# A graph layer on one core: the counts of a chunk's first three banks are made among the last products of the chunk in front of it

## The reference, cut to what matters

```python
N, D, E = 6250, 128, 206250            # nodes, features, edges; dst is sorted
msg = x[src] + edge_attr
agg = jax.ops.segment_sum(msg, dst, num_segments=N)
h = jax.nn.relu(agg @ W1 + b1) @ W2 + b2
h = norm_over_all(h) * ln_w + ln_b      # one mean and variance for the whole of h
h = norm_over_nodes(h) * gn_w + gn_b    # per feature
y = x + jax.nn.gelu(h) + x
out = layernorm(y)                      # per node
...
```

## Time and profile before

| | us |
|---|---|
| median of 3 runs (853.66 to 855.56) | 854.31 |
| profiled execution, its own time | 847.83 |
| its span, first to last instruction | 845.7 |
| one chunk, counts and products | 25.1 |
| of it from first to behind the last of the 98 products | 11.5 |

### The profile page before, as it was taken

One profiled execution on the slowest core, in us unless ns is written; L12 is line 12 of the kernel. 1 busy time (PEld: TensorE's weight loads), 2 busy tenths in 40 slices (PEclk: granted clock), 3 DMA queues, 4 the chain that ended last, 5 costly groups with the idle time before them and its releaser, 6 DMA issues.

```text
span 845.7 us, 25816 instructions
## 1 busy us (share of the span) xinstructions
PE 731.9 (87%) x9449; PEld 616.1 (73%) x9449; DVE 677.6 (80%) x1189; ACT 380.7 (45%) x841; POOL 84.8 (10%) x67
## 2 busy tenths in 40 slices
PE   3566789999999999999999999999999999989840
PEld 3564458777888877888877788877788887778730
DVE  5766678988988988898898898898898898815585
ACT  0120024566444466544466644456644446615464
POOL 1121001011011011011011101111101101000000
PEclk9997769999999999999999999999999999999965
DMA  6759994554334555333555333455433355212005
GB/s 156 276 169 353 359 349 150 158 158 123 113 117 123 155 158 150 101 113 114 154 158 158 116 114 106 139 158 158 130 106 118 122 155 158 80 66 94 0 1 152
DMA packets 88855, 123.45 MB, mean 146 GB/s; under 512 B 8479, under 2 KB 84348, under 8 KB 88635
## 3 DMA queue, kind: packets, MB, share of 16 engines
q1 hardware_dynamic: 78992, 112.83, 42.9%
q0 software_dynamic: 5616, 5.25, 2.2%
q10 hardware_dynamic: 4228, 5.12, 2.0%
HBM read 119.10 MB, written 4.03 MB: 146 GB/s over the span
## 4 chain that ended last, share of the span: by engine, by line
PE 56%; ACT 19%; issue 10%; DMA 8%; DVE 5%; ACTq 1%; DVEq 1%; SPq 0%
PE bank L696 35%; ACT counts L521 17%; DMA edges<-in_edge_attr_dram 6%; PE bank L674 6%; PE bank L623 5%; PE bank L638 3%; PE bank L743 3%; PE bank L753 2%; DMA agg<-in_dst_dram 1%; PE bank L658 1%; ACT sums L491 1%; PE bank L596 1%; DVE pool_m L1192 1%; DVE pool_m L829 1%; ACTq L519 1%
## 5 line engine op out<-in xcount | busy, mean ns | idle before, releaser
L521 ACT CAST counts<-bank 128x490 fp32r<-128x490 f32 x625 | 311.5, 615 | 291.9 <-PE bank L674 289.1
L696 PE MATMUL bank<-counts,x_hi 128*128 128x250 f32 x1225 | 289.1, 281 | 19.6 <-ACT counts L521 19.6
L696 PE MATMUL bank<-counts,x_lo 128*128 128x250 f32 x1225 | 286.5, 279 | 0.0
L696 PEld LDWEIGHTS bank<-counts,x_hi 128*128 128x128 f32 x1225 | 231.3, 189 | 23.5 <-ACT counts L521 23.5
L980 DVE TENSOR_TENSOR pool_m<-listing,turned_lo 128x3328 bf16<-128x3328 bf16 x125 | 235.9, 1887 | 8.4 <-ACT turned_key L501 7.0
L696 PEld LDWEIGHTS bank<-counts,x_lo 128*128 128x128 f32 x1225 | 232.1, 189 | 0.0
L674 PE MATMUL bank<-pool_m 128*128 128x98 bf16 x3125 | 200.8, 209 | 0.0
L674 PEld LDWEIGHTS bank<-pool_m 128*128 128x128 bf16 x3125 | 158.9, 98 | 46.8 <-issue 45.0
L623 PE MATMUL bank<-edges,onehot 128*32 128x128 f32 x3228 | 171.4, 305 | 22.4 <-DMA edges<-in_edge_attr_dram 22.4
L980 DVE TENSOR_TENSOR pool_m<-listing,turned_key 128x2548 bf16<-128x2548 bf16 x125 | 184.7, 1478 | 0.0
L623 PEld LDWEIGHTS bank<-edges,onehot 128*32 128x32 f32 x3228 | 78.4, 117 | 55.9 <-issue 21.8
(11 more groups left out here) (149 smaller groups left out, 414.3 us busy)
## 6 DMA issues: line engine op xcount, KB each, us to landing
edges<-in_edge_attr_dram SPq DMA_DIRECT2D x134, 768.0 KB, 4.6
out_dram<-pool_m SPq DMA_DIRECT2D x6, 512.0 KB
agg<-in_dst_dram SPq DMA_DIRECT2D x1, 768.0 KB
agg<-in_src_dram ACTq DMA_DIRECT2D x1, 768.0 KB
listed<-agg ACTq DMA_DIRECT2D x1, 768.0 KB
begins<-listed,tile_slot POOLq DMA_INDIRECT x27, 5.8
begins<-listed,row_slot POOLq DMA_INDIRECT x27, 3.4
w<-in_L_gnn_W_dram ACTq DMA_DIRECT2D x2, 128.0 KB, 2.2
```

The source lines that it names most:

```text
L521: nc.scalar.copy(counts[:, :, k * nodes:(k + 1) * nodes].rearrange("p q (i m) -> p q i m", m=PAIR), cps[k % RING][:, 0:nodes * NT].rearran ...
L696: last = nc.tensor.matmul(sps[:, 0:CHUNK], part[:, q, :], counts[:, q, :], start=(q == 0 and part is x_hi), stop=(q == NT - 1 and part is ...
```

## The change

PE makes the counts of banks 0, 1 and 2 of chunk c+1 not at the start of that chunk, but in front of the tiles 40, 43 and 46 of the 49 tiles of chunk c's products. The banks are the same three PSUM banks, the waits are the same, and ACT's and DVE's programs are not touched. For the first chunk the three banks are counted ahead of the loop. The last chunk, behind which nothing follows, is written out of the loop.

```diff
+PREFILL_AT = (40, 43, 46)
...
-            def count_chunk(c):
+            def count_bank(c, k):
+                b = k // BPB
+                if k % BPB == 0:
+                    pe.wait_ge(marks_ready, c * BATCHES + (b + 1))
+                if k >= RING:
+                    pe.wait_ge(banks_free, c * BANKS + (k + 1 - RING))
+                for i in range(BANK):
...
+                last.then_inc(banks_done, 1)
+
+            def count_chunk(c, ahead=True):
                 for k in range(BANKS):
...
+                    if k >= len(PREFILL_AT):
+                        count_bank(c, k)
                     if k in PARTS_AT:
...
                 for q in range(NT):
+                    if ahead and q in PREFILL_AT:
+                        count_bank(c + 1, PREFILL_AT.index(q))
                     for part in (x_hi, x_lo):
...
-            with pe.Fori(0, CHUNKS) as c:
+            for k in range(len(PREFILL_AT)):
+                count_bank(0, k)
+            with pe.Fori(0, CHUNKS - 1) as c:
                 count_chunk(c)
+            count_chunk(CHUNKS - 1, ahead=False)
```

More of the change, by code:

```diff
@@ L663, in _ @@
                 round_groups(r)
-            def count_chunk(c):
-                for k in range(BANKS):
[L667 to L679, removed]
+            def count_bank(c, k):
[5 more added lines that the diff above has]
+                for i in range(BANK):
+                    n = (k % BPB) * BANK + i
+                    last = nc.tensor.matmul(cps[k % RING][:, i * KEYS:(i + 1) * KEYS],
+                                            mark_lo[b % MARKED][:, n // INTER, :, n % INTER],
+                                            mark_key[b % MARKED][:, n // INTER, :, n % INTER],
+                                            start=(i == 0), stop=(i == BANK - 1),
+                                            skip_group_check=True)
+                last.then_inc(banks_done, 1)
+            def count_chunk(c, ahead=True):
+                for k in range(BANKS):
+                    if k >= len(PREFILL_AT):
+                        count_bank(c, k)
                     if k in PARTS_AT:
```

## The result

| | before | after |
|---|---|---|
| median of 11 runs, us | 854.31 (852.79 to 856.17) | 858.48 (856.69 to 862.29) |
| profiled execution, its own time | 847.83 | 857.90 |
| span | 845.7 | 855.8 |
| one chunk, mean of 23 | 25.09 | 25.51 |

The change made the kernel slower: ratio 1.0058 (95% interval 1.0041 to 1.0074), 4.2 us by the medians. The two profiled executions are 10.1 us apart. The forecast was 9.6 us more and 863.9, with a range of 857 to 873.

What follows compares the result with a forecast made beforehand. PE was taken to bound the products, ACT the counts with PE nearly a bound. Gaining 0.59 and paying 0.99 us lengthens each of 24 chunks by 0.40: 854.31 + 9.6 = 863.9 us, own range 861 to 867, wide 857 to 873.

Steps and rivals of the forecast that it cites:

- The sum: Whole kernel: each chunk gains 0.59 and pays 0.99, so 0.40 longer; over 24 chunks 9.6 us, giving 863.9.
- the forecast's own range: Kernel time 861 to 867 us, for x from 0.11 to 0.16; chance 0.60.
- the wide range: Kernel time 857 to 873 us, the forecast's own range widened by rivals 1, 2 and 3 to reach 8 in 10.
- rival 1: Product's weight load hidden behind the count products: x = 0.05, 0.16 a chunk, 858.1 us; chance 0.14.
- x: On PE, the step from a group's fifth count product to the next product; taken as 0.13 us, bounds 0.05 to 0.25.
- The price: Three groups of count products among PE's products: 0.33 us each, 0.99 a chunk, bounds 0.75 to 1.35.
- my two middle cases: Product's weight load starts with the last count product (x = 0.11) or once that has streamed (x = 0.16).
- The gain: Counts phase: 0.21 at ACT's first copy and 0.38 over thirteen copies, 0.59 us a chunk; bounds 0.45 to 0.74.
- Passed on whole: After copy 12 the order is untouched, so the whole 0.59 us reaches the next products.
- drained array: Rival 2: the array drains at each return to the products, x = 0.25, 0.76 a chunk, 872.5 us; chance 0.11.
- Rival 3: Among the copies nothing is won; only the start's 0.21 comes through, 0.78 a chunk, 873.0 us; chance 0.05.
- Rival 5: Faster: the pause around bank 14, 0.51 above the pace, goes as well, -0.11 a chunk, 851.7 us; chance 0.04.

Runs made afterwards that it cites:

- the two later comparisons: No edit: the changed kernel timed again against the kernel before on two later occasions; 858.29 us, ratio 1.0119, and 857.50 us, ratio 1.0108.
- the three later occasions: The kernel before, unchanged, timed again on three occasions, each on another chip: 848.64, 848.81 and 848.26 us.
- alone: Against the kernel before, banks 0 to 2 counted among the products and again at the chunk's start, so only the cost is there: 871.57 us, ratio 1.0267.
- the run with the gain alone: Against the kernel before, counts of banks 0 to 2 left out for chunks 1 to 24 (output not the layer's): 836.93 us, ratio 0.9864.

## Why the prediction was right, and where it was off

- **The sum.** Forecast 0.40 a chunk, measured 25.51 - 25.09 = 0.42, in three profiles of the changed kernel. Over 24 chunks 10 us, as the profiles and the two later comparisons (1.0119 and 1.0108, so 9 to 10 us) have it. The first comparison's 4.2 us was half of that. The step that it doesn't fit is "854.31 + 9.6": the median that I added to was 5 to 6 us above what the same kernel took on the three later occasions. I had noted the gap to the profiled 847.83 and took it to be there after the change as well; it was not (858.48 against a profiled 857.90).
- **Luck.** The measured 858.48 lies outside the forecast's own range of 861 to 867. Only the wide range held it, by 1.5 us, and that range reached down to 857 for the sake of rival 1, whose 858.1 is the nearest figure of all although its mechanism (x = 0.05) is ruled out. Had I added to the profiled execution, as the prediction also did (857.4), or to the later medians (848.3 to 848.8, so 857.9 to 858.4), the mechanism would have given the measured time. The mechanism is borne out by the chunks; that 858.48 lay in the range is owed in part to luck.
- **The price.** 0.99 forecast, 0.95 measured, alone and in the changed kernel. The group was 0.20 + x with x = 0.13; x is 0.11, the lower of my two middle cases, which takes off 0.06 for three groups, and the step out of the products is 0.13 (450.20 to 450.33) in place of 0.12, which gives about 0.03 back. The rule of the Trainium skill on the load ("TensorE: Matmul & The Clock Gate", section "LDWEIGHTS (loading the stationary operand)") gave 0.107 for this step: the trace agrees, with 0.11. Its other rule, in the section "What overlaps and what doesn't" (a load overlaps only matmuls in other row groups), doesn't hold here: the product's load starts at 450.53 beside the last count product, in the same full array.
- **The gain.** 0.59 forecast, 0.53 measured: the first copy 0.40 behind the last product in place of 0.36 (before 0.57), and the thirteen copies in 6.41 in place of 6.39 (before 6.77). ACT needs 0.12, not 0.08, from the end of the last product (453.52 to 453.64). The 0.04 for the wait can be had from rows (bank 0 done at 422.22 + 0.41 = 422.63, its copy at 422.67); for the register operation's 0.04 I had none.
- **Passed on whole.** Right in the changed kernel: the time from copy 12 to copy 14 and the last eleven copies are unchanged. Where the chunk gets shorter than 24.68 us it is not whole, as the run with the gain alone showed: DVE's own loop takes that long, and 0.07 of the mean went to it. I had 0.9 us of cover for bank 20 and didn't ask how long DVE's loop is when it waits for nobody. One reading led me wrong there: I took DVE's add of the chunk to follow the last product by 0.75. The gap of 1.29 ahead of the add is the same 1.30 when nothing is waited for; in the changed kernel, where PE is later, the gap is 1.75 and the add stands 0.26 behind the product's end. For this change nothing hung on it.
- **The rivals.** Hidden load (x = 0.05) and drained array (x = 0.25) are both out, by PEld's rows. Rival 3, that only the start's 0.21 comes through, is out by the 6.41 us of the thirteen copies. Rival 5, a pause around bank 14 that goes away, was rightly put down for this change. But the pause could be had cheaply: moving one turn won 0.42 of the 0.51 that the rival put it at.

## What to carry to other kernels

In this kernel, work moved into a phase in which one engine is busy without a gap cost its full length there, and more: 0.95 us, where the phase that it left was rid of 0.69 on PE and gave back 0.53, because ACT was nearly as busy. Ask both questions before such a move: what the work costs among its new neighbours, and how much of its old time the next engine lets through. Before work is moved between phases, look for a pause in which two engines wait for each other in turn (ACT's copy, PE's turn, the next bank): putting the next two banks ahead of the turn won 1.3% with no work moved between the phases at all. A group of small matmuls among large ones paid each time for the way back, the load of the large one's weights. And find out how long each engine's loop is by itself: DVE's 24.68 us stood close below the chunk's 25.09, and the kernel before gave it away only by a wait of 0.26 for ACT.

## What the runs showed of the hardware

- A float32r weight load of 128 columns takes 0.11 us until its matmul streams (450.53 to 450.64 in the changed kernel), and runs beside a bf16 matmul ahead of it; with 98 columns to stream and a step of 0.05 that hides 0.05 of it.
- The chunk 0 of one program took 25.10 us in one profile and 27.60 in another, with the granted clock over 120 to 126 us at 0.89 in the first and at 0.50 (1.2 GHz) in the second. The kernel before took 854.3 us on one occasion and 848.3 to 849.3 on three, while the changed one took 857.5 to 858.5 on all three of its own. What lies behind the first figure is open.
